# Second expert layer: two wide-and-narrow products in place of three, and another order of work on ACT and DVE

## What is computed

```python
probs = softmax(layernorm(x) @ gate_w + gate_b); idx = argmax(probs)
# up to C rows go to each of 8 experts
hmid = relu(einsum('ecd,edf->ecf', buf, w1) + b1[:, None, :])      # 256 -> 1024
ybuf = einsum('ecf,efd->ecd', hmid, w2) + b2[:, None, :]           # 1024 -> 256
y = nan_to_num(ybuf[idx, pos] * prob, posinf=1e4, neginf=-1e4);  x = x + y
```

## Time and profile before

| | |
|---|---|
| timed runs | 1434.73, 1435.18, 1437.02 us, median 1435.18 |
| span of the profiled execution, the slowest core's | 1438.1 us |
| PE busy, whole span | 1225.2 us (85%), 7872 products |
| PEld (weight loads) | 1073.0 us (75%) |
| DVE busy | 1006.2 us (70%) |
| ACT busy | 957.1 us (67%) |
| POOL busy | 1022.2 us (71%) |
| mean granted clock of PE | 0.931 |

### The profile page before, as it was taken

How to read it: one execution, slowest core, us unless ns; L and a number is a source line. 1 busy time by engine, 2 the same in 40 slices (tenths; PEclk the granted TensorE clock), 3 DMA queues, 4 the chain that set the end, 5 groups by cost and what they waited for, 6 DMA issues and landing times.

```text
span 1438.1 us, 26842 instructions
## 1 busy us (share of the span) xinstructions
PE 1225.2 (85%) x7872; PEld 1073.0 (75%) x7872; DVE 1006.2 (70%) x2153; ACT 957.1 (67%) x2128; POOL 1022.2 (71%) x920
## 2 busy tenths in 40 slices
PE   2477768888799245999999999999999999999993
PEld 0244444555555135999999999999999999999993
DVE  7999996987799893756657555755755575556652
ACT  4788896886467353767767666766766776667672
POOL 7788688885787105777768766777776777768785
PEclk9977777999899586999999999999999999999997
DMA  9889986453867003433433322423432342233333
GB/s 327 240 265 284 280 203 163 67 75 45 227 214 261 6 10 96 104 47 48 107 47 80 79 45 45 110 44 52 107 48 44 48 110 48 44 49 56 51 54 40
DMA packets 132130, 153.55 MB, mean 107 GB/s; under 512 B 17410, under 2 KB 118850, under 8 KB 131926
## 3 DMA queue, kind: packets, MB, share of 16 engines
q0 software_dynamic: 51648, 64.60, 27.6%
q1 hardware_dynamic: 58758, 66.60, 14.2%
q10 hardware_dynamic: 21648, 21.49, 4.5%
HBM read 98.83 MB, written 53.81 MB: 106 GB/s over the span
## 4 chain that ended last, share of the span: by engine, by line
PE 55%; issue 3%; POOL 2%; ACT 1%; DMA 1%; DVE 0%; ACTq 0%; POOLq 0%; DVEq 0%
PE f_ps_y L1636 27%; PE f_ps_h L1624 26%; PE f_ps_x L1614 2%; POOL out L1515 1%; POOL xg L1497 1%; POOL sg L1501 0%; DMA sg<-stat_rows,idx_row 0%; ACT h_all L1564 0%; ACT h_hi L1563 0%; ACT y_all L1574 0%; ACT f_xn L1548 0%; DMA out<-clean,put_now 0%; DMA sg<-stat_rows,idx_now 0%; DVE clean L1701 0%; DVE x_lo L1669 0%
## 5 line engine op out<-in xcount | busy, mean ns | idle before, releaser
L1563 ACT ACTIVATE h_hi<-f_ps_h,c_b 128x384 fp32r<-128x384 f32 (+1 forms) x416 | 237.1, 570 | 262.9 <-PE f_ps_h L1624 262.9
L1674 DVE TENSOR_TENSOR h_lo<-h_all,h_hi 128x768 fp32r<-128x768 f32 (+1 forms) x208 | 184.2, 886 | 256.6 <-ACT h_all L1564 256.1
L1636 PE MATMUL f_ps_y<-w_hi,h_hi 128*128 128x256 f32 x1136 | 325.2, 286 | 0.0
L1636 PE MATMUL f_ps_y<-w_lo,h_hi 128*128 128x256 f32 x1136 | 320.1, 282 | 0.0
L1636 PE MATMUL f_ps_y<-w_hi,h_lo 128*128 128x256 f32 x1136 | 320.0, 282 | 0.0
L1515 POOL DMA_INDIRECT out<-clean,put_now x159 | 262.8, 1653 | 57.5 <-issue 49.1
L1497 POOL DMA_INDIRECT xg<-out,idx_now x159 | 192.7, 1212 | 128.5 <-issue 118.3
L1624 PE MATMUL f_ps_h<-x_hi,w_hi 128*128 128x384 f32 (+1 forms) x832 | 271.9, 327 | 8.0 <-issue 3.5
L1624 PE MATMUL f_ps_h<-x_lo,w_hi 128*128 128x384 f32 (+1 forms) x832 | 269.3, 324 | 0.0
L1624 PE MATMUL f_ps_h<-x_hi,w_lo 128*128 128x384 f32 (+1 forms) x832 | 269.0, 323 | 0.0
L1564 ACT ACTIVATE h_all<-f_ps_h,c_b 128x384 f32<-128x384 f32 (+1 forms) x416 | 238.1, 572 | 0.0
(11 more groups left out here) (227 smaller groups left out, 2280.7 us busy)
## 6 DMA issues: line engine op xcount, KB each, us to landing
shared<-out SPq DMA_DIRECT2D x40, 512.0 KB, 4.0
w_raw<-in_w SPq DMA_DIRECT2D x16, 1024.0 KB, 7.2
xin<-in_x SPq DMA_DIRECT2D x24, 512.0 KB, 7.0
out<-xin ACTq DMA_DIRECT2D x24, 512.0 KB, 5.2
shared<-in_x SPq DMA_DIRECT2D x16, 512.0 KB, 5.5
out<-shared ACTq DMA_DIRECT2D x16, 512.0 KB, 5.7
dst_row<-in_dst SPq DMA_DIRECT2D x20, 256.0 KB, 4.7
xg<-out,idx_now POOLq DMA_INDIRECT x159
```

What stands on the lines that cost most here:

```text
L1563: nc.scalar.activation(h_hi[:, f, :n * P], ps_h[:, f % SLOTS, :n * P], ACT.Relu, bias=b1[:, e, f:f + 1])
L1636: ins = nc.tensor.matmul(ps_y[:, i], x[:, f, i * P:(i + 1) * P], weights[s][:, w], start=i != 1 and f == 0 and n == 0, stop=f == KF - 1 an ...
L1674: tt(h_lo[:, pair, :n * P], h_all[j % 2][:, :, :n * P], h_hi[:, pair, :n * P].bitcast(F32), ALU.subtract).then_inc(h_lo_ready, 1)
```

## The change

The second layer's weights get a layout of their own, `down[s][:, f, 0]` high and `down[s][:, f, 1]` low, so that one product of 512 columns computes high by high and high by low, and a second one of 256 columns adds low by high to the latter half. `ps_y` grows from two PSUM banks to three, and `ps_h` shrinks from four slots to three. DVE sums the two halves and the bias in two steps, and does the scaling by the probability as well, as a third step; ACT no longer does it. ACT does its eight relus of a block without a break, and normalises after them. The transposes come after j = 1 and not j = 0. ACT makes all high cuts of the weights, six ahead of relu 0 and two after `take_high`; DVE makes only low ones, two in each of j = 0 to 2 and two after `take_low`.

```diff
-        self.hi = [sb(f"w_hi{s}", F32R) for s in range(2)]
-        self.lo = [sb(f"w_lo{s}", F32R) for s in range(2)]
+        self.up_hi = [half(f"w_up_hi{s}", [P, self.W1]) for s in range(2)]
+        self.up_lo = [half(f"w_up_lo{s}", [P, self.W1]) for s in range(2)]
+        self.down = [half(f"w_down{s}", [P, HID // P, 2, D]) for s in range(2)]
...
-    SLOTS = 4
+    SLOTS = 3
-    BY_ACT = 4
+    AHEAD = 6
...
-        ps_y = ps("f_ps_y", [P, 4, D])
+        ps_y = ps("f_ps_y", [P, BT, 2, D])
...
             def step(e, b, n, split=None):
+                if split is not None:
+                    for c in range(AHEAD):
+                        weights.split_high(nc, act, e + 1, split, c)
                 for f in range(KF):
                     relu(e, b, f, n)
-                    if f == 1:
-                        scale_rows(b - 1)
-                    if f == 3:
-                        act.wait_ge(turned, b + 1)
-                        act.sem_inc(spare_act, 1)
-                        normalise(b + 1)
-                        act.wait_ge(prob_ready, b + 2)
-                        act.sem_inc(spare_act, 1)
-                        keep_prob()
-                    if split is not None and f >= KF - BY_ACT:
-                        weights.split_high(nc, act, e + 1, split, f - (KF - BY_ACT))
+                act.wait_ge(turned, b + 1)
+                act.sem_inc(spare_act, 1)
+                normalise(b + 1)
+                act.wait_ge(prob_ready, b + 2)
+                act.sem_inc(spare_act, 1)
+                keep_prob()
                 take_high(b + 1)
+                if split is not None:
+                    for c in range(AHEAD, CUTS):
+                        weights.split_high(nc, act, e + 1, split, c)
...
             def up(b, s, f, tiles):
-                pe.wait_ge(h_taken, KF * b + (f + 1))
+                pe.wait_ge(h_taken, KF * b + (f + 1 if f >= SLOTS else SLOTS))
...
                     for f in (2 * j, 2 * j + 1):
-                        w = slice(W1 + f * D, W1 + (f + 1) * D)
-                        for n, (x, weights) in enumerate(((h_hi, w_hi), (h_hi, w_lo), (h_lo, w_hi))):
-                            ins = nc.tensor.matmul(ps_y[:, i], x[:, f, i * P:(i + 1) * P], weights[s][:, w],
-                                                   start=i != 1 and f == 0 and n == 0,
-                                                   stop=f == KF - 1 and n == 2 and i > 0)
+                        nc.tensor.matmul(ps_y[:, i], h_hi[:, f, i * P:(i + 1) * P], w_down[s][:, f],
+                                         start=f == 0, stop=False)
+                        ins = nc.tensor.matmul(ps_y[:, i, 1], h_lo[:, f, i * P:(i + 1) * P], w_down[s][:, f, 0],
+                                               start=False, stop=f == KF - 1)
...
-                    if j == 0:
+                    if j == 1:
                         turn(b + 1)
...
                     if split is not None:
-                        for c in (2 * j, 2 * j + 1):
-                            if c < CUTS - BY_ACT:
-                                weights.split_own(nc, v, tt, e + 1, split, BY_ACT + c, (CUTS - BY_ACT) * e + c + 1)
-                            else:
-                                a = c - (CUTS - BY_ACT)
-                                weights.split_low(v, tt, e + 1, split, a, CUTS + BY_ACT * e + a + 1)
+                        for c in range(2 * j, min(2 * j + 2, AHEAD)):
+                            weights.split_low(v, tt, e + 1, split, c, CUTS * e + CUTS + c + 1)
                 take_low(b + 1)
+                if split is not None:
+                    for c in range(AHEAD, CUTS):
+                        weights.split_low(v, tt, e + 1, split, c, CUTS * e + CUTS + c + 1)
                 add_infinities(b - 1)
                 keep_finite(b - 1)
                 v.wait_ge(y_ready, b + 1)
-                tt(y_sum[:, :n], ps_y[:, :n], b2[:, bass.ds(e, 1)].broadcast_to([P, n, D]),
-                   ALU.add).then_inc(y_sum_ready, 1)
+                tt(y_sum[:, :n], ps_y[:, :n, 1], b2[:, bass.ds(e, 1)].broadcast_to([P, n, D]),
+                   ALU.add).then_inc(y_step, 1)
+                v.wait_ge(y_step, 3 * b + 4)
+                v.sem_inc(spare_dve, 1)
+                tt(y_sum[:, :n], ps_y[:, :n, 0], y_sum[:, :n], ALU.add).then_inc(y_sum_ready, 1)
+                v.wait_ge(y_sum_ready, b + 2)
+                v.sem_inc(spare_dve, 1)
+                tt(y_all[:, :n], y_sum[:, :n], prob[:, :n].unsqueeze(2).broadcast_to([P, n, D]),
+                   ALU.mult).then_inc(y_step, 2)
```

More of the change, by code:

```diff
@@ L1360, in sb, with half @@
             return ctx.enter_context(nc.sbuf_tensor(name, [P, self.COLS], dt))
+        def half(name, shape):
+            return ctx.enter_context(nc.sbuf_tensor(name, shape, F32R))
         self.raw = sb("w_raw", F32)
-        self.hi = [sb(f"w_hi{s}", F32R) for s in range(2)]
-        self.lo = [sb(f"w_lo{s}", F32R) for s in range(2)]
+        self.up_hi = [half(f"w_up_hi{s}", [P, self.W1]) for s in range(2)]
+        self.up_lo = [half(f"w_up_lo{s}", [P, self.W1]) for s in range(2)]
+        self.down = [half(f"w_down{s}", [P, HID // P, 2, D]) for s in range(2)]
         self.raw_in = [ctx.enter_context(nc.semaphore(f"raw_in{n}")) for n in range(2)]
@@ L1367, in __init__ @@
         self.lo_ready = ctx.enter_context(nc.semaphore("lo_ready"))
-        self.hi_own = ctx.enter_context(nc.semaphore("hi_own"))
         self.spare = ctx.enter_context(nc.semaphore("w_spare"))
@@ L1384, in load, with raw_cut, half_cut @@
                      self.w2[e]).then_inc(self.raw_in[1], 16)
-    def cut(self, n):
-        return slice(n * self.CUT, (n + 1) * self.CUT)
+    def raw_cut(self, n):
+        raw = self.raw[:, n * self.CUT:(n + 1) * self.CUT]
+        return raw if n < self.W1 // self.CUT else raw.rearrange("p (f c) -> p f c", c=D)
+    def half_cut(self, s, n, low):
+        if n < self.W1 // self.CUT:
+            return (self.up_hi, self.up_lo)[low][s][:, n * self.CUT:(n + 1) * self.CUT]
+        f = (n * self.CUT - self.W1) // D
+        return self.down[s][:, f:f + self.CUT // D, low]
     def split_high(self, nc, act, e, s, n):
         act.wait_ge(self.raw_in[n * self.CUT // self.W1], 16 * e + 16)
-        nc.scalar.copy(self.hi[s][:, self.cut(n)], self.raw[:, self.cut(n)]).then_inc(self.hi_ready, 1)
+        nc.scalar.copy(self.half_cut(s, n, 0), self.raw_cut(n)).then_inc(self.hi_ready, 1)
     def split_low(self, engine, tensor_tensor, e, s, n, highs):
@@ L1396, in split_low @@
         engine.sem_inc(self.spare, 1)
[L1397 to L1404, removed]
+        tensor_tensor(self.half_cut(s, n, 1), self.raw_cut(n), self.half_cut(s, n, 0).bitcast(F32),
                       ALU.subtract).then_inc(self.lo_ready, 1)
@@ L1410, in expert_block @@
     KJ = KF // 2
-    SLOTS = 4
-    W1 = weights.W1
+    SLOTS = 3
     CUTS = weights.CUTS
-    BY_ACT = 4
+    AHEAD = 6
     with ExitStack() as ctx:
@@ L1423, in sem @@
             return ctx.enter_context(nc.semaphore(name))
-        w_hi, w_lo = weights.hi, weights.lo
+        w_hi, w_lo, w_down = weights.up_hi, weights.up_lo, weights.down
         hi_ready, lo_ready = weights.hi_ready, weights.lo_ready
@@ L1468, in expert_block @@
         y_sum_ready = sem("y_sum_ready")
-        y_all_ready = sem("y_all_ready")
+        y_step = sem("y_step")
         parts_ready = sem("parts_ready")
@@ L1486, in _ @@
             for e in range(1, NEXP):
-                sp.wait_ge(hi_ready, CUTS + BY_ACT * (e - 1))
+                sp.wait_ge(hi_ready, CUTS * e)
                 sp.wait_ge(lo_ready, CUTS * e)
@@ L1565, in relu @@
                                      bias=b1[:, e, f:f + 1]).then_inc(h_taken, 1)
-            def scale_rows(b):
-                act.wait_ge(y_sum_ready, b + 2)
-                act.wait_ge(prob_ready, b + 2)
-                act.wait_ge(parts_ready, 3 * b + 6)
-                act.wait_ge(clean_ready, b + 2)
-                act.sem_inc(spare_act, 1)
-                for i in range(BT):
-                    ins = nc.scalar.activation(y_all[:, i], y_sum[:, i], ACT.Copy, scale=prob[:, i:i + 1])
-                ins.then_inc(y_all_ready, 1)
             act.sem_inc(h_taken, SLOTS)
@@ L1605, in _ @@
                     step(e, b, BT)
-            scale_rows(end - 1)
         @block.tensor
@@ L1678, in next_prob @@
                 v.wait_ge(prob_next_ready, b + 1)
-                v.wait_ge(y_all_ready, b + 1)
+                v.wait_ge(y_step, 3 * b + 3)
                 v.sem_inc(spare_dve, 1)
@@ L1683, in find_infinite @@
             def find_infinite(b):
-                v.wait_ge(y_all_ready, b + 2)
+                v.wait_ge(y_step, 3 * b + 6)
                 v.wait_ge(clean_ready, b + 2)
@@ L1701, in keep_finite @@
                 nc.vector.copy_predicated(clean[:], finite[:], y_all[:]).then_inc(clean_ready, 1)
-            nc.vector.memset(prob[:], 0.0).then_inc(prob_ready, 1)
```

(2 more changed lines are left out.)

4 lines of the change are left out of this document (1 added, 3 removed).

## The result

The changed kernel takes 1450.16 us (median of 4 runs, 1446.41 to 1455.53), the one before 1436.1 (4 runs, 1434.73 to 1437.24). The ratio is 1.0084, 95% interval [1.0058, 1.011]: slower by 0.8%, about 12 us. (The ratio is an estimate over the runs and not the quotient of the two medians, which are 14 us apart.) Forecast were 1447.2 us and "slower", so direction and size came out. Several terms of the sum did not, as the trace shows.

What follows compares the result with a forecast made beforehand. TensorE bounds the expert blocks, busy 846.84 of 858 us. Terms +0.35 + 4.6 + 4.5 + 1.0 + 0.25 + 1.2 - 3.2 + 3.3 give +12.0 us: 1450.1 profiled, 1447.2 timed; range 1441 to 1452.

Steps and rivals of the forecast that it cites:

- The products: Second layer: 512 plus 256 columns replace three 256-column products, saving 4.4 ns a pair; -3.2 us over 32 wide blocks.
- rival 1: Second layer: the excess over 2.4 GHz stays fixed, 225.4 ns for 512 columns; +4.3 us, 1439.5 us; chance 0.15.
- Three slots just do when the relus are unbroken: First layer: unbroken relus free three ps_h slots in time, so TensorE never stops for them; narrow first layer gains 0.45 us.
- Rival 3: Ordinary wide blocks: three slots, or lateness carried between blocks, stop TensorE there too; +9.5 us more, 1456.7 us; chance 0.14.
- DVE decides: Block starts: DVE's longer chain delays both splits, hence relus 4 and 6 and the transposes; some 10 us of f_xn waits.
- Rival 2: Blocks' starts: DVE's later turns, relu 6 behind split 1, don't reach TensorE; about -7 us, 1428 us; chance 0.12.
- First narrow blocks at +0.05: Seven narrow blocks following wide ones: later transposes give back the 0.45 us gain; +0.05 us each, +0.35 in all.
- Second and third narrow blocks and the wide ones after a run: Late DVE chain and waits for POOL's adds: second narrow +4.6, third +1.2, wide ones 4.5 + 1.0 + 0.25 us.
- The tail: After the last product: later normalising delays the last gathering and the adds behind it; +3.3 us.

Runs made afterwards that it cites:

- runs with three slots: The kernel before with ps_h cut from four slots to three and nothing else: 1541.83 us, ratio 1.0718 to the kernel before.
- the products alone: The kernel before with 512- and 256-column products, three ps_y banks, three ps_h slots and two DVE sums, ACT's order as before: 1527.2 us, ratio 1.0622.
- three products again: The changed kernel with the 512-column product split again into two of 256 columns in the same bank: 1457.75 us, ratio 1.0135 to the kernel before.
- bounds run: The changed kernel with DVE reading the next expert's block bounds inside the first wide block, ahead of take_low: 1443.87 us, ratio 1.0043 to the kernel before.
- two small mends: On the changed kernel: bounds read early on DVE, last POOL gathering left out; with tests and scaling behind split 1 too, 1421.6 us, ratio 0.988.

## Why the prediction was right, point by point

- **The products** gain little since the columns stay the same: right in kind. The term was mis-sized, with 4.4 ns a pair forecast and 6.5 to 7.6 measured, -5.7 us instead of -3.2 in the ordinary wide blocks. The line through two pitches gave 233.2 ns, the wide product takes 230 to 231. The excess over 2.4 GHz is 12.1, 16.0 and 16.7 to 17.4 ns at 256, 384 and 512 columns: it flattens. The fixed excess of rival 1 isn't there either. The Trainium skill ("TensorE: Matmul & The Clock Gate", section "Back-to-back issue gap") gives N/2.4 + 2.5 ns for a product by itself, from which 215.8 is the estimate for 512 columns; the trace shows 230 and decides.
- **Three slots just do when the relus are unbroken, and not otherwise.** Right: there is no wait for a slot in ordinary wide blocks, and the runs with three slots or the products alone show the price of broken relus. Rival 3, stops in ordinary wide blocks, did not come: they are all at 17.5.
- **DVE decides, by relu 4 behind split 0 and relu 6 behind split 1.** Right, and shown by moving the tests. Rival 2 (these waits not reaching TensorE) is refuted for the change: TensorE waits 10.4 us for relus and 12.2 for `f_xn`, where some 10 were forecast. Only with another order on DVE do these waits nearly go.
- **First narrow blocks at +0.05.** This is the step that failed. "The three operations end at 2.7, so split 0 goes when relu 1 is done": they ended at 3.37, since `y_sum` started 0.20 after the block's start and not 0.45 before it, as TensorE no longer pauses ahead of the block. Then DVE's loads at the change of expert took 1.29 us, a term that the sum did not have; they had lain in idle time before. Split 0 went at 4.66 instead of 2.78, and the seven blocks cost 8.2 us instead of 0.35. The lost pause alone costs little, as it is time gained ahead of the block (three products again). The loads are the cause: read elsewhere, the blocks are 13.04 long. From relu 6 on, the working holds: transposes 3.18 us after it for 3.20. A slip beside it: the terms as written add up to 12.63 and not 12.68, which would have made this +0.
- **Second and third narrow blocks and the wide ones after a run** were put at +11.55 and measured +6.5. The mechanism is there (DVE waits 2.4 us for the adds in the second narrow block at 775.46), but only one of the three wide blocks after a pair, of 19.5 us, had the lateness in full; the others had 18.0 and 18.5, and the ones after the run of three and in the last expert 17.7 and 17.5. A likely reason for the smaller sum is that with longer first blocks POOL had more time than I gave it. The bounds run supports that: with first blocks of 13.04 us `put_now` waits 0.3 us in them, and the second ones are longer. Why only one of the three was late in full is not shown; its first blocks were as long as the others'.
- **The tail** came as forecast, +3.8 for +3.3, and by the mechanism named, since leaving out the gathering takes it away. The third add is issued 8.5 us after the last product's start and not 4.9, 3.7 later.

The forecast total was right in part by luck, because errors stood against each other: 8 us of loss too little at the first narrow blocks, against 5 us of loss too much in the blocks behind them and 2.5 us of gain too little in the products.

## What to carry to other kernels

When work moves onto an engine that is not the bottleneck, look for what that engine does unseen at a loop's edge: register loads show as no busy time in the profile, and here they became a delay once they no longer fell into idle time. A buffer given up (four slots to three) has to be weighed with the order of work of the engine that frees it; here one without the other cost 6 to 7%. And in an in-order engine, put what others wait for ahead of what nobody needs soon: the same change with tests and scaling behind split 1 and with two small mends is 1.2% faster than the kernel before, not 0.8% slower. Not all of these 17 us are the wide products': the run with three products puts them at 5 to 8 us, and leaving out the last gathering would, by the estimate above, give the kernel before some 2 us too. Whether the new order alone, with three products and all four slots, does as well was not run.

## What the runs showed of the hardware

- At a granted clock of 1.00 the distance of two products of this type, each with its own weight load, is 118.8 ns for 256 columns, 176.0 for 384 and 230 to 231 for 512.
- With one instruction pair less in three, TensorE's pause of 0.65 us at each new expert is gone; with three products it is back. With three slots and ACT's old order it is the same: a pause with the old products, none with the wide ones. That its instructions run further ahead of the array then would explain it, but no run took that apart.
- DVE's three register loads at a new expert show as a pause of 1.2 to 1.3 us, which the profile puts down to a semaphore satisfied two microseconds before its end.
